# One-hot columns of the routing table on ScalarE, and phases that end without GpSimd's drain

## The reference

```
x = x + 0.5 * ffn(layernorm(x))
x = x + attn(layernorm(x))
x = x + 0.5 * ffn(layernorm(x))

def attn(X):      # 16 heads of 16 numbers
    KVc = cumsum over the positions of outer(K, V)
    Y = einsum(Q, KVc), then a small matrix per head, then Wc

def ffn(x):       # E = 8 experts, K = 2 of them for a token, F = 1024
    top_v, top_i = top_k(clip(x @ Wr), K)
    top_p = softmax(top_v)
    pos = the token's place in its expert's list; kept = pos < cap (2560)
    h = silu(xe @ W1) * (xe @ W3);  ye = h @ W2
    out[tokens] += top_p * kept * ye
```

## Time and profile before

| | |
|---|---|
| time, median of 3 runs | 2999.72 us (2999.57 to 2999.74) |
| the profiled execution, own time | 3000.1 us |
| its span, first to last instruction | 2998.4 us |
| mean granted TensorE clock | 0.973 of full speed |
| PE busy | 2840.5 us, 95% of the span |
| DVE, ACT, POOL busy | 1617.6 us, 1274.0 us, 1167.4 us |
| route phase, to the first matmul of e1 | 153.5 us, PE busy 65.35 |
| e1 and e2 | some 1147 and 1155 us, PE busy 1142 in each |
| middle, first to last of its work | 525.6 us, PE busy 490.69 |

### The profile page before, as it was taken

The page is one execution under the profiler, slowest core; times in us unless marked ns, Lnnn a source line. Parts: engine busy times, 40 slices in busy tenths (PEclk is TensorE's granted clock), DMA queues, the critical chain, the costliest instruction groups (busy, mean ns, idle before and its releaser), DMA issues. The chain is left out here.

```text
span 2998.4 us, 54774 instructions
## 1 busy us (share of the span) xinstructions
PE 2840.5 (95%) x18723; PEld 2543.4 (85%) x18723; DVE 1617.6 (54%) x3791; ACT 1274.0 (42%) x2685; POOL 1167.4 (39%) x1550
## 2 busy tenths in 40 slices
PE   4399999999999999979999995999999999999998
PEld 3389899989999989868888884998999998899987
DVE  8844445455454545447877876445545454545443
ACT  5244444444344434334444443344434343444443
POOL 3754444444444434310211122443444543444433
PEclk8699999999999999989999997999999999999999
DMA  7542323232332322120112013322323231323212
GB/s 248 183 126 34 84 35 81 41 78 39 83 70 48 83 36 36 36 55 30 59 50 67 30 44 94 85 43 71 86 36 78 43 84 30 81 41 78 43 34 29
DMA packets 155114, 197.23 MB, mean 66 GB/s; under 512 B 15536, under 2 KB 127024, under 8 KB 154928
## 3 DMA queue, kind: packets, MB, share of 16 engines
q0 software_dynamic: 62688, 87.11, 17.2%
q1 hardware_dynamic: 81952, 97.30, 9.9%
q10 hardware_dynamic: 10288, 10.38, 1.0%
HBM read 124.32 MB, written 78.79 MB: 68 GB/s over the span
## 5 line engine op out<-in xcount | busy, mean ns | idle before, releaser
L1267 DVE TENSOR_TENSOR e_h_lo<-e_hid,e_h_hi 128x384 fp32r<-128x384 f32 (+1 forms) x640 | 384.4, 601 | 399.0 <-ACT e_h_hi L1228 391.6
L1264 DVE TENSOR_TENSOR e_hid<-e_ps,e_gate 128x384 f32<-128x384 f32 (+1 forms) x640 | 381.5, 596 | 373.4 <-ACT e_gate L1224 364.0
L1228 ACT ACTIVATE e_h_hi<-e_hid 128x384 fp32r<-128x384 f32 (+1 forms) x640 | 356.8, 558 | 422.6 <-DVE e_hid L1264 417.5
L1224 ACT ACTIVATE e_gate<-e_ps 128x384 f32<-128x384 f32 (+1 forms) x640 | 333.8, 522 | 407.9 <-PE e_ps L102 399.9
L100 PE MATMUL e_ps<-e_xT_hi,e_wb 128*128 128x384 f32 (+1 forms) x1280 | 456.5, 357 | 0.0
L101 PE MATMUL e_ps<-e_xT_lo,e_wb 128*128 128x384 f32 (+1 forms) x1280 | 455.0, 355 | 0.0
L102 PE MATMUL e_ps<-e_xT_hi,e_wb 128*128 128x384 f32 (+1 forms) x1280 | 454.9, 355 | 0.0
L100 PE MATMUL e_ps<-e_xT_hi,c_wa 128*128 128x384 f32 (+1 forms) x1280 | 451.2, 353 | 2.5 <-DVE e_xT_lo L1256 2.5
L102 PE MATMUL e_ps<-e_xT_hi,c_wa 128*128 128x384 f32 (+1 forms) x1280 | 449.4, 351 | 0.0
L101 PE MATMUL e_ps<-e_xT_lo,c_wa 128*128 128x384 f32 (+1 forms) x1280 | 449.2, 351 | 0.0
L438 POOL DMA_INDIRECT c_xrow<-normed_rows,e_token x320 | 346.6, 1083 | 155.7 <-issue 83.8
(11 more groups left out here) (297 smaller groups left out, 4767.3 us busy)
## 6 DMA issues: line engine op xcount, KB each, us to landing
c_raw<-w SPq DMA_DIRECT2D x204, 256.0 KB
normed_rows<-r_xn SPq DMA_DIRECT2D x8, 1056.0 KB, 7.0
normed_rows<-mi_xn SPq DMA_DIRECT2D x8, 1056.0 KB, 4.7
x<-x ACTq DMA_DIRECT2D x8, 1024.0 KB, 12.3
out<-mi_x SPq DMA_DIRECT2D x8, 1024.0 KB, 5.3
r_xin<-x SPq DMA_DIRECT2D x7, 1024.0 KB, 10.9
c_raw<-x SPq DMA_DIRECT2D x7, 1024.0 KB, 8.5
c_xrow<-normed_rows,e_token POOLq DMA_INDIRECT x320
```

The costliest lines, as they stand in the source:

```text
L1224: act.activation(gate[:, f % 2, 0:n], ps1[f % 2][:, 0:n], ACT.Silu).then_inc(gated, 1)
L1228: act.activation(h[0][:, f, 0:n], hid[:, f % 2, 0:n], ACT.Copy).then_inc(h_high, 1)
L1264: dve.tensor_tensor(hid[:, f % 2, 0:n], ps3[f % 2][:, 0:n], gate[:, f % 2, 0:n], ALU.mult).then_inc(hid_ready, 1)
L1267: dve.tensor_tensor(h[1][:, f, 0:n], hid[:, f % 2, 0:n], h[0][:, f, 0:n].bitcast(F32), ALU.subtract).then_inc(h_ready, 1)
```

## The change

Seven things change.

1. **Columns by ScalarE.** ACT makes picked_col of quads 5, 9, 13 and 15 in route and of the last quad in the middle. It has no equality test, so it takes two instructions for one of DVE's: the distance of each column number from the token's (`Abs`), then `Relu(code - code * distance)`, which is the code where the distance is zero and zero elsewhere. That makes 16 activations of 128x160 for a quad in place of DVE's eight. In route they stand behind the copies and weight pieces of the group, ahead of the next group's `front`. DROPPED becomes 1e4, and minus_code is made once.
2. **No drain.** All four blocks are told to leave out POOL's drain. Where something behind the block relies on it, there are waits now: route waits for its low parts, the expert phases for their adds.
3. **x loaded from e1.** The four loads of x of line 451 are issued by SP at e1's end, once the adds have landed, instead of at the middle's start.
4. **Moments in two parts.** The middle's first moments are made for chunks 0 and 1 alone, then for the other six; the first mi_vpad waits for the first part alone.
5. **`weigh` later.** In the middle ACT's exponential moves from the head of step c = 2 to its end.
6. **Columns ahead of the additions** in steps c = 5 and 6 of the middle's last group with attention.
7. **First turn.** In the expert phases PE's first turn waits for four gathers instead of three.

```
+    def pick_cols_by_scalar(self, act, g, b, q, i, far):
+        act.wait_ge(self.placed, g + 1)
+        wait(act, self.tabled, q + 1 - self.ring)
+        for c in range(QUAD):
+            for j in range(TOPK):
+                ins = act.activation(far[:, c * TOPK + j, :], self.k.steps[:], ACT.Abs, scale=-1.0,
+                                     bias=self.colf[b][:, i * QUAD + c, j:j + 1])
+        ins.then_inc(self.k.far_ready, 1)
+        act.wait_ge(self.k.far_ready, self.scalar_at + self.scalar_cols(q) + 1)
+        for c in range(QUAD):
+            at = q * QUAD + c
+            for j in range(TOPK):
+                ins = act.activation(self.picked_col[:, self.ring_at(q) + c, j, :], far[:, c * TOPK + j, :], ACT.Relu,
+                                     scale=self.k.minus_code[:, at:at + 1], bias=self.k.code[:, at:at + 1])
+        ins.then_inc(self.k.scalar_cols_ready, 1)
...
+        by_scalar = tuple((b + n) * NB // QUAD - 1 for b, n in GROUPS[1:])
...
-        with nc.Block() as block:
+        with nc.Block(no_gpsimd_drain=True) as block:
...
                     for q in WEIGHTS[g]:
                         high_w(q)
+                    for i in quads(g):
+                        if quad(g, i) in by_scalar:
+                            act.wait_ge(su.centered, 1)
+                            r.pick_cols_by_scalar(act, g, g % 2, quad(g, i), i, far)
...
                     for i in quads(g):
-                        r.pick_cols(dve, g, g % 2, quad(g, i), i)
+                        if quad(g, i) not in by_scalar:
+                            r.pick_cols(dve, g, g % 2, quad(g, i), i)
...
+                if phase == 0:
+                    sp.wait_ge(w_low, PIECES * (E + 1))
+                    sp.wait_ge(all_added, 1)
+                    ahead.load_x1(sp, rows_of(raw), groups_of(acc))
...
-                if phase == 1:
-                    ahead.wait_added(pool, k, n, phase)
+                wait_alone(pool, y_added, WORDS * n + 16 * SMALL, k.passed)
+                if phase == 0:
+                    pool.nop().then_inc(all_added, 1)
...
-                turn(16 * SMALL, SMALL)
+                turn(WORDS, SMALL)
...
-                sp.wait_ge(ahead.all_added, 1)
-                ahead.load_x1(sp, x1, x1_g)
...
-                ahead.wait_added(pool, k, pool.value_load(tiles_in.first[0:1, E:E + 1], min_val=3 * E, max_val=E * MAX_TILES), 0)
-                pool.nop().then_inc(ahead.all_added, 1)
...
-                    if c == 0:
-                        act.wait_ge(n1_ready, g + 1)
+                    if n == 0:
+                        act.wait_ge(n1_ready, 1)
+                    if n == 2 or c == 0 and g >= 1:
+                        act.wait_ge(n1_ready, g + 2)
...
                 for n in STEPS:
                     g, c = divmod(n, MG)
-                    if c == 2 and g >= 1:
-                        r.weigh(act, g - 1, MG)
...
+                    if c == 2 and g >= 1:
+                        r.weigh(act, g - 1, MG)
+                    if c == 6 and g == MGS:
+                        r.pick_cols_by_scalar(act, g - 1, (g - 1) % 2, MQ * g - 1, 1, far)
...
-                for c in range(MG):
+                for c in range(2):
                     stats_x1(0, c)
-                moments_x1(0)
+                moments_x1(0, 0, 2)
+                for c in range(2, MG):
+                    stats_x1(0, c)
+                moments_x1(0, 2, MG)
...
+                    last = g == MGS - 1
+                    if c in (5, 6) and last:
+                        r.pick_cols(dve, g - 1, (g - 1) % 2, MQ * (g - 1) + c - 5, c - 5)
                     if chunk(n):
                         add_out(n)
                         stats_x2(n)
```

More of the change, by code:

```diff
@@ L66 @@
 CLAMP = 10000.0
-DROPPED = 1.0e6
+DROPPED = 1.0e4
 TAKEN = 1.0e9
@@ L347, in pick_cols, with scalar_cols @@
         ins.then_inc(self.cols_ready, 1)
+    def scalar_cols(self, q):
+        return sum(p < q for p in self.by_scalar)
+    def pick_cols_by_scalar(self, act, g, b, q, i, far):
[13 more added lines that the diff above has]
+        ins.then_inc(self.k.scalar_cols_ready, 1)
     def tabulate(self, pe, q, first, last):
@@ L430, in __init__ @@
         self.rows_loaded = [m.sem(f"rows_loaded{i}") for i in range(2)]
-        self.y_added = [m.sem(f"y_added{i}") for i in range(2)]
-        self.all_added = m.sem("all_added")
         self.x_first = [m.sem(f"x1_first{i}") for i in range(MG // 2)]
@@ L551, in numbers @@
         dve.tensor_scalar(k.even[:], k.parity_i[:, 0:1], 0.5, None, ALU.is_lt)
+        dve.drain()
+        dve.tensor_scalar(k.minus_code[:], k.code[:], -1.0, None, ALU.mult)
         dve.drain()
@@ L992, in expert_phase @@
         h = [m.sb("h_hi", [P, KF, WIDE], F32R), m.sb("h_lo", [P, KF, WIDE], F32R)]
-        yrow, y_added = ahead.yrow, ahead.y_added[phase]
+        yrow = m.sb("yrow", [P, BIG, D])
         ps1 = [m.ps(f"ps1_{b}") for b in range(2)]
@@ L1013, in expert_phase @@
         y_kept = m.sem("y_kept")
+        y_added = m.sem("y_added")
+        all_added = m.sem("all_added") if phase == 0 else None
         w_high = m.sem("w_high")
@@ L1666, in _ @@
                         r.place_rest(dve, (g - 1) % 2, MQ * (g - 1), xn2[:, (g - 1) % 2, :, D:DX])
-                    if c in (5, 6) and g >= 1:
-                        r.pick_cols(dve, g - 1, (g - 1) % 2, MQ * (g - 1) + c - 5, c - 5)
+                    if c in (5, 6) and g >= 1 and not last:
+                        if MQ * (g - 1) + c - 5 not in by_scalar:
+                            r.pick_cols(dve, g - 1, (g - 1) % 2, MQ * (g - 1) + c - 5, c - 5)
                         if g == MGS:
```

45 lines of the change are left out of this document (26 added, 19 removed).

## The result

The changed kernel takes 2969.58 us (median of 4 runs, 2969.14 to 2969.86), against 2999.73 us before: 30.2 us less, a ratio of 0.9899 with an interval of 0.9882 to 0.9916. The forecast was 2973.4.

The account below looks back on a forecast made before the run. It took PE to fill nearly all of e1 and e2 and DVE to be busiest in route. Gains summing to 26.3 us took 3000.1 to 2973.8, and 0.4 less for the runs' median gave 2973.4; range 2966 to 2983.

Parts of the forecast that it names:

- 1, the columns: Route: moving columns from DVE to ACT, 6.1 us per sixteen activations, has the table read earlier; 3.6 us gained.
- S: Route: start of POOL's rows for group 3, at 115.00 us before and forecast at 114.0.
- the copies' issue ending when it did: Route: case where ACT's copy issue ends no earlier, putting S at 118.4 and changing route by +0.8 us.
- 2, gathers before e1 and e2: Boundaries into e1 and e2: without the drain PE's first turn starts earlier, 0.6 us gained at each.
- 3, from e1 into the middle: Boundary from e1 to the middle: x loads issued at 1302.85 and no drain let PE start 4.8 us earlier.
- 4, the moments: Middle's start: splitting moments removes the scale wait, 2.5 us, and a higher clock for second projections gives 1.6.
- 5, `weigh`: Middle: moving the exponential to its step's end removes PE's wait for mi_qT in seven groups, 5.6 us gained.
- 6, the tail: Middle's tail: columns ahead of additions gain 1.3 us, and ACT making quad 15's columns gains 0.7.
- 7, the end: Program's end: without POOL's drain the span ends 5.0 us earlier, or nothing if what runs afterwards waits as long.
- ACT as the bound up to S: Rival, route: copies' issue ends when it did, route loses 0.8 us instead of gaining 3.6; 2978 us, chance 0.2.
- The drain's time: Rival, program's end or e1's end: removing the drain does not gain its 5 us; 2978 to 2980 us, chance 0.2.
- A slower outcome: Rival: an activation costs far more than 0.52 us, above 0.93 the gain is lost, at 1.2 3013 us; chance 0.02.

Follow-up runs that it names:

- run 11: Changed kernel with quad 9's columns made by DVE and those of quads 5, 13 and 15 still by ACT: 2967.25 us.
- run 1: Kernel before with only the drain removed, the waits this needs, and first turns waiting for four gathers: 2990.02 us.
- run 3: Changed kernel with DVE making all columns again, in route and in the middle's last group: 2976.39 us.
- run 5: Changed kernel in which SP, in e2 alone, waits for the first four gathers to land before issuing its weight loads: 2966.35 us.
- run 6: Changed kernel in which POOL, in e2 alone, waits for the first four gathers to land before its memset of e_yrow: 2969.04 us.
- run 8: Changed kernel with the middle's first moments in one piece for all eight chunks: 2974.08 us.
- run 4: Changed kernel with the exponential (`weigh`) back at the head of step c = 2: 2977.28 us.
- run 12: Changed kernel with POOL's default drain restored at the end of e2 alone, the program's last block: 2975.58 us.
- run 7: Changed kernel with group 2's three block copies of x issued with group 3's, behind group 4's `front`: 2975.18 us.
- run 10: Changed kernel with e2's weight loads held behind four gathers, copies of x spread differently, and quad 15's columns on DVE: 2967.14 us.
- run 2: Changed kernel with the default drain restored at the end of all four blocks: 2976.64 us.

## Why the prediction was right, step by step

**1, the columns.** The price was right (5.98 against 6.1), and so was the place: quad 9's activations stand ahead of group 4's `front`, and run 11 shows that they hold S up there. That S came out at 114.2 where 114.0 was forecast is luck: it lies at 113.7 to 115.0 with all columns on DVE (before, runs 1 and 3) and at 113.6 to 115.7 with ACT's help, so the forecast 1.0 us cannot be seen. The Trainium skill, "ScalarE: Activation LUTs", section "What ACT_TABLE_LOAD costs", gives an estimate of 5.9 us for the sixteen. The trace agrees with 5.98. The rule of the same page to use VectorE, not ScalarE, for relu (the Trainium skill, section "Rules for kernel authors") is borne out for quad 9 (run 11) and not for all the quads together (run 3). Mis-sized was the stretch behind S, 23.5 instead of 24.7: I gave the last tables the 1.25 us that they took after a wait of 1.9, and they hardly wait now. In the other executions with this route it is 23.5 to 24.2, against 27.9 to 28.4 with all columns on DVE, and this is where the gain lies. The 0.6 taken off for new operations was not to be seen. One sum in the prediction is slightly off, without effect on the forecast: with the copies' issue ending when it did, S is 114.0 + 2.2 + 2.5 = 118.7 and not 118.4.

**2, gathers before e1 and e2.** Right before e1, wrong before e2. The failed step is that the turn "starts some 0.6 earlier, and again before e2": before e2 it came 3.5 later. I took the landing time of a gather from stretches in which SP loads nothing, and asked of the drain only what POOL waits for, not what the barrier behind it holds back on SP. Runs 5 and 6 show that it is SP's twelve weight loads.

**3, from e1 into the middle.** The 4.8 us came, but not from where the step put them. It reasoned that "the loads are then issued by SP at 1302.85", so from the move. Run 1 has the whole gain with the loads where they were. The barrier was what waited, and the sum was right because both edits were in it. The prediction's case of a barrier that needs only the adds' landing is the one that came true.

**4, the moments.** Right in mechanism, too large for the split. The two terms (2.5 and 1.6) are 4.1, and undoing the split costs 2.9 us up to the third chunk's projections. The row's 5.2 has 2.3 more that came with the drain and the earlier loads (runs 1 and 8). The wait of 2.70 for the scale had in it DVE's waits for loads of x, 0.56 us and, in the kernel before,

```profile
1314.50 0.75 DVE L152 BATCH_NORM_STATS2 mi_n_stats<-c_raw 128x6 f32<-128x256 f32 x2 [1.21 <-DMA c_raw<-x]
```

**5, `weigh`.** Right in place, mis-sized: -5.6 forecast, 7.7 when undone. I counted the listed waits. A step that is late by 0.8 cost over 1.0 in each group, since PE is busy for longer with the same matmuls as well (run 4).

**6, the tail.** The additions' move gave the 1.3 forecast, by subtraction and not by a run of its own: `weigh` is 7.6 of that piece's 8.9 (run 4). The wait for the columns fell by 2.5, and a new one of 0.8 appeared, of PE for DVE's addition, which now stands behind them. The end gave its 0.7 between the last two tables, but the piece 2.2. ACT's columns are 1.0 of it (32.3 in run 3). In the rest PE's matmuls behind the late table take less time (0.71 for eight where they took 1.23, after a wait of 1.18 instead of 3.71): the granted clock of the 8 us from the late table's start is 0.92, where it was 0.71. This piece was 34.3 us in run 1 and 33.5 before with the same code there, so that some 0.8 of it may be spread.

**e1's 1.3** were not forecast and cannot be put down to the change. They go with the granted clock of e1's first 10 us: 0.56 before and 0.71 in the changed kernel, with 1.00 in the rest of e1 in both. But run 6, whose e1 has the same code, shows 0.59 and 1146.71 us, and run 8 shows 0.70 and 1145.49.

**7, the end.** Right: 4.7, and run 12 shows that it is part of the time.

**The rivals.** ACT as the bound up to S was real (runs 7 and 11), but the issue of the copies ended 5.3 us earlier than before, so that the rival's price did not fall due. The drain's time was to be had. A slower outcome had no price near it: an activation took 0.33 or 0.42. The forecast missed by 4.1 before e2 and by some 8 the other way over the other pieces; it came as close as it did because the two have opposite signs. Without the miss before e2 the time would have been some 2965.5 by this sum, just below the range.

## What to carry to other kernels

A barrier holds back every engine's next program, not only the one whose drain it waits for; before taking it away, list what the others start at once, and hold back the transfers that compete with the one the first matmul needs (here 3.2 us, run 5). Work moved to a less busy engine should be placed by what is queued behind it there: here quad 9's columns stood ahead of the next group's work, and giving them back to the busier engine gained 2.4 us. A wait that recurs in every group is worth at least what the list shows for it. Runs 5 and 11 touch different pieces; together they would give about 2964 us by their sum, which was not run; run 10 shows that such sums can fail, since an earlier table ran into another wait.

## What was not expected of the hardware

- Behind four gathers the default drain at a block's end cost 0.7 us (2.6 us from issue to turn, 1.9 without), but behind adds with accumulation 4.7 to 5.4 us, at the end of e1 and of e2. In runs 2 and 12 these came on top of a wait for the landing of the adds.
- PE's turn came 1.8 to 2.1 us behind the issue of the last of four gathers where SP's loads started behind it, and 4.5 to 6.4 us behind it where twelve loads of 256 KB started ahead of the fourth.
- The issue of block copies of 1 MB on ACT's queue took 1.3 to 2.4 us for two, 2.9 to 7.3 for three, 7.9 for four and 17.2 for six, each time with ACT doing nothing else.
- PE's second projections in the middle took 3.78 us behind waits of 2.80 and 0.47, 3.46 behind 1.34 and 0.47, and 2.05 behind 0.47 alone, in three kernels that differ little. The granted clock in the first case was 0.50 of full speed, the lower of its two levels (1.2 GHz), and 1.00 in the third.
